# One regrouping transfer per pair instead of per duo, the last pair divided on two engines, half of the last FFN input later, and new orders

## The reference, cut to what matters

```
xn  = layernorm(x)
xa  = layernorm(xn) * ln_w + ln_b
q, k, v = xa @ W_q + b_q, xa @ W_k + b_k, xa @ W_v + b_v      # 16 heads of 64
p   = softmax(causal(q k^T / 8))                               # 256 x 256 per head
att = concat(p v) @ W_o + b_o
ffn = relu(xn @ tern(W1)^T + b1) @ tern(W2)^T + b2             # 512 hidden, weights -1, 0, 1
out = x + att + ffn
```

## Time and profile before

| | us |
|---|---|
| median of 3 runs | 224.38 (223.8 to 224.81) |
| the profiled execution, its own time | 225.33 |
| its span in the trace | 223.5 |
| PE busy | 211.9 (95%) |
| VectorE busy | 201.8 (90%) |
| ScalarE busy | 195.5 (87%) |
| GpSimd busy | 184.8 (83%) |

### The profile page before, as it was taken

The page is one execution under the profiler, slowest core; times in us unless marked ns, Lnnn a source line. Parts: engine busy times, 40 slices in busy tenths (PEclk is TensorE's granted clock), DMA queues, the critical chain, the costliest instruction groups (busy, mean ns, idle before and its releaser), DMA issues.

```text
span 223.5 us, 9672 instructions
## 1 busy us (share of the span) xinstructions
PE 211.9 (95%) x3670; PEld 187.9 (84%) x3670; DVE 201.8 (90%) x776; ACT 195.5 (87%) x733; POOL 184.8 (83%) x363
## 2 busy tenths in 40 slices
PE   7999799999999999999998999989999999999795
PEld 5766498888998899889987999879998998899584
DVE  3499999999999999999999999999999999999931
ACT  0999999997999899997999899997999899996830
POOL 5799989999988989798988899797988985996530
PEclk9999999999999999999999999999999999999999
DMA  5990656606675487636855566636756567677700
GB/s 155 279 273 6 141 116 172 143 3 144 146 158 127 105 196 174 133 78 153 172 134 150 123 147 159 121 84 143 173 119 177 109 152 171 153 165 161 165 5 23
DMA packets 24030, 30.79 MB, mean 138 GB/s; under 512 B 2608, under 2 KB 23088, under 8 KB 23984
## 3 DMA queue, kind: packets, MB, share of 16 engines
q1 hardware_dynamic: 23840, 30.16, 57.5%
q10 hardware_dynamic: 144, 0.02, 0.0%
HBM read 4.73 MB, written 1.05 MB: 26 GB/s over the span
## 4 chain that ended last, share of the span: by engine, by line
PE 46%; ACT 16%; DVE 14%; POOL 11%; DMA 7%; SPq 3%; issue 2%; POOLq 0%; DVEq 0%
PE s_ps L822 8%; DMA pT<-blocks 7%; PE m_ps L862 7%; ACT prob L491 5%; DVE s_ps L603 4%; ACT prob L493 4%; PE m_ps L940 4%; DVE blocks L616 3%; SPq L351 3%; PE m_ps L787 3%; POOL prob L315 3%; ACT qk L480 2%; PE m_ps L789 2%; PE m_ps L788 2%; ACT qk L482 2%; POOL prob L314 2%
## 5 line engine op out<-in xcount | busy, mean ns | idle before, releaser
L491 ACT ACTIVATE prob<-s_ps,neg_max 128x256 f32<-128x256 f32 x128 | 67.6, 528 | 5.6 <-DVE neg_max L603 5.2
L315 POOL TENSOR_SCALAR prob<-prob,inv_sum 128x256 f32<-128x256 f32 x126 | 61.3, 486 | 0.0
L616 DVE STREAM_TRANSPOSE blocks<-prob 128x768 f32<-128x768 f32 x62 | 59.7, 968 | 1.6 <-POOL prob L315 1.6
L314 POOL TENSOR_SCALAR prob<-prob,inv_sum 128x128 f32<-128x128 f32 x126 | 47.5, 377 | 15.4 <-DVE inv_sum L610 15.4
L603 DVE CUSTOM_DVE_ANT_0 s_ps<-s_ps,causal 128x256 f32<-128x256 f32 x128 | 55.1, 430 | 5.0 <-PE s_ps L822 4.5
L493 ACT ACTIVATE prob<-s_ps,neg_max 128x128 f32<-128x128 f32 x128 | 54.0, 422 | 0.0
L862 PE MATMUL m_ps<-pT,v 64*64 64x64 f32 (+2 forms) x1536 | 49.0, 256 | 3.5 <-DMA pT<-blocks 2.1
L822 PE MATMUL s_ps<-qk 64*64 64x128 f32 (+2 forms) x1280 | 49.9, 276 | 0.9 <-ACT prob L493 0.5
L862 PEld LDWEIGHTS m_ps<-pT,v 64*64 64x64 f32 x1536 | 42.5, 133 | 8.8 <-DVE zT_lo L622 3.6
L822 PEld LDWEIGHTS s_ps<-qk 64*64 64x64 f32 x1280 | 42.0, 133 | 7.1 <-issue 3.8
L603 DVE CUSTOM_DVE_ANT_0 s_ps<-s_ps,causal_first 128x128 f32<-128x128 f32 x128 | 42.4, 331 | 0.0
(11 more groups left out here) (120 smaller groups left out, 492.4 us busy)
## 6 DMA issues: line engine op xcount, KB each, us to landing
pT<-blocks SPq DMA_DIRECT2D x124, 192.0 KB, 3.6
xT_cur<-in_xT SPq DMA_DIRECT2D x8, 128.0 KB, 4.2
outT<-out_sb SPq DMA_DIRECT2D x8, 128.0 KB, 4.0
x_all<-in_x SPq DMA_DIRECT2D x1, 768.0 KB, 8.6
wv_raw<-in_w_v SPq DMA_DIRECT2D x2, 256.0 KB, 5.5
wo<-in_w_o SPq DMA_DIRECT2D x1, 512.0 KB, 6.5
x_all<-in_x SPq DMA_DIRECT2D x2, 128.0 KB, 3.9
wq_raw<-in_w_q SPq DMA_DIRECT2D x2, 128.0 KB, 2.5
```

The source lines that it names most:

```text
L314: op(first, first, inv_sum[:, j, 2 + h:3 + h], 0.0, ALU.mult, ALU.add)
L315: last = op(later, later, inv_sum[:, j, h:h + 1], 0.0, ALU.mult, ALU.add)
L491: nc.scalar.activation(later, s_ps[:, pair % 2, h, 0:S].rearrange("p (g j k) -> p g j k", g=TILES, j=QT), ACT.Exp, bias=neg_max[:, j, h:h ...
L616: nc.vector.transpose(blocks[:, duo, :, n, :, :], prob[:, pair % NBUF, :, :, :, :] .rearrange("p h j g k -> p (j g) h k")).then_inc(turned, 1)
```

## The change

Three edits of structure, and new order strings for all five queues.

**A transfer for each pair.** `blocks` and `pT` are laid out by pair instead of by duo, `pT_in` has 8 semaphores, and `regroup(b, pair)` waits for its own pair's turning and issues 4 DMAs of 128 runs of 768 bytes, 96 KB each. A batch then has 32 regrouping DMAs with the same bytes in all. `turn_blocks` waits for its own pair's transfer of the batch before, and `y` waits for both pairs' semaphores. The wait on `z_psd` is the duo's, as before.

**The last pair's division.** `divide_on_vector` (`q7` on VectorE) divides head 0 alone, in 2 instructions, and a new step `q7` on ScalarE, `divide_on_scalar`, divides head 1 in 2 instructions. `tw7` and `tn` wait for both.

**The last FFN input.** In batch 7 `oa` takes hidden chunks 0 and 1 (4 products) and waits for the first half of `h` alone; chunks 2 and 3 enter at the head of `ob`, with the wait for the second half. The number of products is the same.

```diff
-        blocks = sb("blocks", [P, DUOS, QT * 3, 2, 2, QB])
-        pT = sb("pT", [P, DUOS, QT, 3, 2, 2, QB])
+        blocks = sb("blocks", [P, PAIRS, QT * 3, 2, QB])
+        pT = sb("pT", [P, PAIRS, QT, 3, 2, QB])
...
-            def regroup(b, duo):
-                wait(sp, turned, PAIRS * b + 2 * duo + 2)
-                wait(sp, z_psd, 4 * (DUOS * (b - 1) + duo + 1))
+            def regroup(b, pair):
+                wait(sp, turned, PAIRS * b + pair + 1)
+                wait(sp, z_psd, 4 * (DUOS * (b - 1) + pair // 2 + 1))
                 for i in range(QT):
                     rows = slice(i * QB, i * QB + QB)
-                    sp.dma_start(pT[:, duo, i, :, :, :, :].rearrange("p g n h q -> p (g n h q)"),
-                                 blocks[rows, duo, :, :, :, :].rearrange("k c n h q -> k (c n h q)")
-                                 .rearrange("k (j r) -> k j r", j=QT)).then_inc(pT_in[duo], 16)
+                    sp.dma_start(pT[:, pair, i, :, :, :].rearrange("p g h q -> p (g h q)"),
+                                 blocks[rows, pair, :, :, :].rearrange("k c h q -> k (c h q)")
+                                 .rearrange("k (j r) -> k j r", j=QT)).then_inc(pT_in[pair], 16)
...
+            def divide_on_scalar(b, pair):
+                wait(act, inv_ready, PAIRS * b + pair + 1)
+                j = pair % NBUF
+                for cols, col in ((slice(0, P), 3), (slice(P, W), 1)):
+                    part = ordered(pair, 1)[:, cols]
+                    last = nc.scalar.activation(part, part, ACT.Copy, scale=inv_sum[:, j, col:col + 1])
+                last.then_inc(last_prob_by_scalar, 1)
...
-                        pe.wait_ge(pT_in[duo], 16 * QT * (b + 1))
+                        for pair in (2 * duo, 2 * duo + 1):
+                            pe.wait_ge(pT_in[pair], 16 * QT * (b + 1))
...
+            def hidden_into(dst, chunks, clears):
+                for hid in (hT_hi, hT_lo):
+                    for c in chunks:
+                        nc.tensor.matmul(dst, w2T[:, c, :], hid[:, c, :], start=(clears and hid is hT_hi and c == 0), stop=False)
...
-                wait(pe, h_ready, 2 * b + 2)
-                for hid in (hT_hi, hT_lo):
-                    for c in range(FC):
-                        nc.tensor.matmul(dst, w2T[:, c, :], hid[:, c, :], start=(hid is hT_hi and c == 0), stop=False)
+                if b < B - 1:
+                    wait(pe, h_ready, 2 * b + 2)
+                    hidden_into(dst, range(FC), True)
+                else:
+                    wait(pe, h_ready, 2 * b + 1)
+                    hidden_into(dst, range(FC // 2), True)
...
+                if b == B - 1 and duos.start == DUOS // 2:
+                    wait(pe, h_ready, 2 * b + 2)
+                    hidden_into(dst, range(FC // 2, FC), False)
```

**The orders.** The strings of SP and of the repeated and last batch for VectorE, and the tails of ScalarE and TensorE, before and after:

```diff
-DVE_PLAN = ("i7- m0 m1 ln+ m2 z0- t7- m3 i0 m4 m5 z1- i1 t0 v0 m6 i2 m7 z2- m8 m9 v1 t1 i3 m10 m11 z3- v2 t2 m12 "
-            "xh+ t3 i4 m13 i5 v3 m14 m15 t4 i6 t5 xn+ o- t6")
+DVE_PLAN = ("m1 t6- m2 z0- ln+ i0 m3 t7- m4 z1- m5 i1 v0 m6 m7 i2 m8 z2- m9 v1 t0 m10 m11 i3 z3- t1 i4 v2 xh+ m12 "
+            "t2 v3 i5 m13 t3 t4 m14 i6 m15 m0+ t5 xn+ o- i7")
-DVE_TAIL = ("... i5 m13 t4 o- t5 i6 m14 m15 z0 v2 i7 v3 q7 z1 n3 z2 z3 o")
+DVE_TAIL = ("... v1 t4 t5 o- m14 m15 z0 v2 i6 v3 i7 q7 z1 n3 z2 z3 o")
-ACT_TAIL = ("... z0 e14 e15 f0 z1 w6 f1 w7 z2 z3")
+ACT_TAIL = ("... z0 e14 e15 f0 q7 f1 z1 w6 w7 z2 z3")
-PE_TAIL = ("... x1:1 f0:2 y1:0 z1 tw6:3 f1:2 tw7:3 x2:0 tn3:2 y2:1 x3:2 z2 y3:3 z3 oa:1 ob oc")
+PE_TAIL = ("... f0:2 x1:1 y1:0 f1:3 z1 tw6:2 tn3:3 tw7:2 x2:0 y2:1 z2 x3:3 y3:2 z3 oa:0 ob oc")
-SP_HEAD = ("d0 d1 d2 d3 d0+ d1+ d2+ d3+ d0++ st d1++")
-SP_PLAN = ("d2 d3 st- d0+ d1+")
-SP_TAIL = ("d2 st- st")
+SP_HEAD = ("d0 d1 d2 d3 d4 d5 d6 d7 d0+ d1+ d2+ d3+ d4+ d5+ d6+ d7+ st d0++ d1++ d2++ d3++")
+SP_PLAN = ("d4 d5 d6 d7 d0+ st- d1+ d2+ d3+")
+SP_TAIL = ("d4 d5 st- st")
```

More of the change, by code:

```diff
@@ L48 @@
 BUSY = (5, 1)
-PE_HEAD = ("xb:2 pr0:3 pr1:0 xn:2 s0 pr2:1 pr3:0 s1 v0:3 s2 v1:2 ta:3 pr4:0 pr5:1 s3 pr6:3 v2:2 s4 pr7:3 f0:0 s5 "
[3 rows of a table removed]
[L53 to L64, removed]
@@ L74 @@
-POOL_PLAN = ("h0- p7- h1- p0 p1 ln+ p2 p3 xl+ p4 p5 p6")
-POOL_TAIL = ("p7- p0 h0- p1 h1- p2 p3 p4 p5 p6 h0 h1")
-SP_HEAD = ("d0 d1 d2 d3 d0+ d1+ d2+ d3+ d0++ st d1++")
-SP_PLAN = ("d2 d3 st- d0+ d1+")
-SP_TAIL = ("d2 st- st")
+PE_HEAD = ("xb:0 pr0:0 pr1:1 xn:3 s0 pr2:0 s1 v0:2 v1:3 ta:1 pr3:2 s2 v2:0 pr4:3 pr5:2 s3 pr6:0 s4 pr7:2 v3:0 "
[3 rows of a table added]
+PE_PLAN = ("x0-:2 y0-:1 s1 z0- pr4:3 pr5:0 x1-:2 y1-:1 s2 z1- v0:3 pr6:0 x2-:1 y2-:2 s3 z2- s4 pr7:0 v1:3 x3-:1 "
+           "y3-:2 s5 z3- s6 v2:3 v3:0 xh+:2 oa-:1 f0:3 pr0+:2 pr1+:0 f1:3 s7 s0+ xn+:2 ob- pr2+:0 pr3+:3")
@@ new lines @@
+PE_TAIL = ("x0-:1 pr4:2 y0-:0 s1 x1-:3 z0- y1-:2 s2 z1- x2-:1 y2-:0 s3 z2- pr5:3 pr6:2 s4 v0:3 x3-:2 pr7:0 y3-:1 "
+           "s5 z3- s6 oa-:3 v1:0 ob- x0:1 y0:2 s7 z0 v2:0 v3:3 f0:2 x1:1 y1:0 f1:3 z1 tw6:2 tn3:3 tw7:2 x2:0 "
+           "y2:1 z2 x3:3 y3:2 z3 oa:0 ob oc")
+ACT_HEAD = ("wh0 wh1 pr0 wh2 pr1 xn wh3 e0 aa pr2 e1 e2 e3 pr3 e4 wh4 pr4 e5 pr5 pr6 e6 e7 pr7 xh+ e8 e9 xn+ f0 "
+            "e10 f1 e11 pr0+ e12 e13 pr1+ z0 pr2+ e14 e15 e0+ e1+ pr3+ z1 e2+ pr4+ e3+ pr5+ wh5 e4+ z2 e5+ oh "
+            "pr6+ e6+ e7+ pr7+ z3 e8+ xh++ e9+ e10+ e11+ f0+ f1+ e12+ pr0++ e13+ xn++ e14+ pr1++")
@@ new lines @@
+ACT_PLAN = ("e15- pr2 pr3 e0 z0- e1 pr4 e2 pr5 z1- e3 e4 e5 pr6 z2- e6 e7 e8 e9 pr7 z3- e10 xh+ e11 e12 f0 pr0+ "
+            "e13 pr1+ f1 xn+ e14")
+ACT_TAIL = ("e15- e0 pr2 pr3 pr4 e1 z0- e2 e3 z1- e4 e5 z2- pr5 pr6 e6 e7 e8 e9 pr7 e10 z3- e11 e12 e13 z0 e14 "
+            "e15 f0 q7 f1 z1 w6 w7 z2 z3")
+DVE_HEAD = ("lz nh xb m0 m1 xn ln+ wl0 v0 m2 th m3 v1 m4 i0 m5 te0 v2 m6 i1 t0 m7 m8 wl1 i2 m9 i3 v3 t1 m10 xh+ "
[3 rows of a table added]
+DVE_PLAN = ("m1 t6- m2 z0- ln+ i0 m3 t7- m4 z1- m5 i1 v0 m6 m7 i2 m8 z2- m9 v1 t0 m10 m11 i3 z3- t1 i4 v2 xh+ m12 "
+            "t2 v3 i5 m13 t3 t4 m14 i6 m15 m0+ t5 xn+ o- i7")
@@ new lines @@
+DVE_TAIL = ("t6- m1 t7- m2 i0 m3 z0- m4 m5 i1 z1- t0 m6 i2 m7 z2- t1 m8 m9 t2 v0 i3 m10 m11 m12 i4 t3 z3- i5 m13 "
+            "v1 t4 t5 o- m14 m15 z0 v2 i6 v3 i7 q7 z1 n3 z2 z3 o")
+POOL_HEAD = ("hs np wl2 wl3 ln+ p0 wl4 p1 p2 p3 xl+ h0 p4 p5 h1 p6 p7 ln++ wl5 p0+ ol p1+ p2+ p3+ xl++ p4+ p5+ p6+")
+POOL_PLAN = ("h0- p7- p0 ln+ p1 h1- p2 p3 xl+ p4 p5 p6")
+POOL_TAIL = ("p7- h0- p0 h1- p1 p2 p3 p4 p5 p6 h0 h1")
+SP_HEAD = ("d0 d1 d2 d3 d4 d5 d6 d7 d0+ d1+ d2+ d3+ d4+ d5+ d6+ d7+ st d0++ d1++ d2++ d3++")
@@ L203, in attention_ffn_kernel @@
         vec_in = sem("vec_in")
-        pT_in = [sem(f"pT_in{n}") for n in range(DUOS)]
+        pT_in = [sem(f"pT_in{n}") for n in range(PAIRS)]
         out_done = [sem(f"out_done{n}") for n in range(2)]
@@ L226, in attention_ffn_kernel @@
         last_wide = sem("last_wide")
+        last_prob_by_scalar = sem("last_prob_by_scalar")
         out_bias_ready = sem("out_bias_ready")
@@ L546, in _ @@
                     copy_wide(index)
+                elif kind == "q":
+                    divide_on_scalar(b, index)
                 elif kind == "wh":
@@ L613, in turn_blocks @@
                 wait(dve, prob_ready, PAIRS * b + pair + 1)
-                duo, n = divmod(pair, 2)
-                wait(dve, pT_in[duo], 16 * QT * b)
-                nc.vector.transpose(blocks[:, duo, :, n, :, :], prob[:, pair % NBUF, :, :, :, :]
+                wait(dve, pT_in[pair], 16 * QT * b)
+                nc.vector.transpose(blocks[:, pair, :, :, :], prob[:, pair % NBUF, :, :, :, :]
                                     .rearrange("p h j g k -> p (j g) h k")).then_inc(turned, 1)
@@ L631, in divide_on_vector @@
                 j = pair % NBUF
[L632 to L635, removed]
+                for cols, col in ((slice(0, P), 2), (slice(P, W), 0)):
+                    part = ordered(pair, 0)[:, cols]
+                    last = nc.vector.tensor_tensor(part, part, inv_sum[:, j, col:col + 1].broadcast_to(part.shape), ALU.mult)
                 return last
@@ L859, in product @@
                         else:
-                            turned_part = pT[rows, duo, i, tile + queries.start:tile + queries.stop, n, h, :]\
+                            turned_part = pT[rows, 2 * duo + n, i, tile + queries.start:tile + queries.stop, h, :]\
                                 .rearrange("p i g q -> p g i q")
@@ L892, in wait_divided @@
                     pe.wait_ge(last_prob_ready, 1)
+                    pe.wait_ge(last_prob_by_scalar, 1)
                 else:
```

6 lines of the change are left out of this document (1 added, 5 removed), and 12 rows, old and new, of tables (DVE_HEAD, PE_HEAD).

## The result

The changed kernel takes 245.34 us (median of 4 runs, 244.86 to 246.69) against 224.39 for the kernel before on the same chip: ratio 1.094 [1.090, 1.099]. It is 21 us slower. The forecast was 222.2, and the range ended at 228.0. Some executions of a kernel show a lower granted clock and take some per cent longer; ratios compare the others alone.

The account below looks back on a forecast made before the run. It took VectorE and PE as nearly full, VectorE's work of about 24.3 us limiting each batch. Gains 1.3 + 0.7 - 0.3 + 0.5 = 2.2 us off 224.38 gave 222.2 us, range 219.3 to 228.0.

Parts of the forecast that it names:

- Part 1: Regrouping transfers for each pair: pair 7's data land earlier, so `y3` no longer waits; gain 1.3 us.
- I take 2.35: SP's queue: a group of four 96 KB issues takes 2.35 us, with 3.08 kept for the range.
- It just fits: Before `y3`: pair 7's transfer `d7` lands at 34.6 us into the plan, needed at 35.0.
- the rival: SP's queue becomes the bound in every batch: 225.5 to 228 us, full form about 232; chance 0.30.
- The head: Start of the kernel: `wl0` moved behind `ln+`, 0.3 us uncovered; cost +0.3 us, between -1 and +1.5.
- Part 2: New orders in the repeated batches: less VectorE waiting for scores and GpSimd's division; gain 0.7 us, between 0 and 2.1.
- Part 3: The new order at the kernel's start: a loss of 0.3 us, between -1 and +1.5.
- Part 4: The tail: divided pair ready 1.8 us earlier; gain 0.5 us, between 0 and 1.8, a loss if SP is late.
- the sign of its failure: SP's queue: waits for `turned` shrinking from several us to nothing would mean the queue is the bound.

Follow-up runs that it names:

- half the issues: Each pair regrouped in two DMAs of 192 KB (output not the reference's): in the changed kernel 222.56 us, in the kernel before with its own orders 223.76 us.
- Early landings alone: The kernel before with its own orders, each pair regrouped by itself in two DMAs of 192 KB (output not the reference's): 223.76 us, ratio 0.996.
- the tail's experiment: The kernel before with only pair 7's division shared by VectorE and ScalarE and the late FFN half, PE's order as before: 224.14 us, ratio 0.9973.

## Why the prediction was wrong

**Two steps failed. The first is the first term of Part 1, "I take 2.35" us for a group of four issues.** It rested on four issues at the price of the first one, 0.54. But 0.54 is the first issue of a group; one behind another takes 0.60 (median 605 ns of 248). The earlier trace rows had the median, 616 ns, and the prediction quoted only the smallest. A group is 2.51 without any hold, 2.81 on the average of the run, and 2.76 to 3.06, gaps included, on the average of the seven in a row. The half that was right: the growth of the issues to 1.1 us within a group was a backlog, and with 96 KB it is gone.

**"It just fits"** was then a sum without room: `d7` landing at 34.6 where 35.0 was the need. It named its own limit, 2.5 us a group, and the median measured is 2.51 (the shortest 2.48, the mean 2.81).

**The second step is the overlap: the rival was the case, but its price was too small.** It decided from 2.94 us a group, eight groups and SP's other work in 25.2 us. The groups measured, 2.90 on the average of the four rows of the loop, stay below that, and by the prediction's own rule they give 225.5 to 228, not 245. The old orders with the same transfers come near that (229.5), though by the first two batches and the end and not by waits in each. The rule treats SP as an engine with a share of work, and has nothing for a new order in which SP's work waits for `y3` and `y3` for SP's work. The loop decides earlier: from `y3` to pair 1's issue 4.3 us at best, seven groups, 1.9 to the next `y3`. It fits 25.2 us up to (25.2 - 4.3 - 1.9) / 7 = 2.71 us a group. At 3.0 it gives 27.2, and with 5.8 instead of 4.3 it gives 28.7: 2 to 3.5 us a batch, not the 1.2 of the prediction (the rows of the loop have 0.3 to 3.0). The difference is the part that waits for SP and then makes SP wait: PE takes its steps in order, and the scores behind `y3` and VectorE's `z3-` ahead of `t1` stand behind the landing.

**The head** was costed at +0.3, between -1 and +1.5; it lost 8.3. SP issues from 25.14 to 46.1 without a pause in batch 0 and from 57.55 to 78.25 in batch 1: the prediction counted SP's work in the repeated batches only. With half the issues the head has nothing of it: `y3` of batches 0 and 1 comes at 44.9 and 70.8, 0.7 and 1.0 us sooner than before.

**The sum of the gains was right for a kernel whose queue is free, in part by luck.** Early landings alone bring 0.9 us (224.68 x (1 - 0.9958)), forecast 1.3. The tail's edits bring 0.6, forecast 0.5. All together bring 224.68 x (1 - 0.9919) = 1.8, forecast 2.2; if the gains add, which no run shows, 0.3 is left for the orders and the head, forecast 0.4. But it doesn't lie where it was forecast. By the table above the new orders bring nothing in the repeated batches (99.9 us against 99.3), where Part 2 had 0.7, and 1.2 us up to `y3` of batch 1 (70.8 against 72.0), where Part 3 had a loss of 0.3.

**The tail** went as told up to the divided pair. VectorE and ScalarE in the changed kernel, then PE:

```profile
230.61 0.84 ACT L503 ACTIVATE prob<-prob,inv_sum 128x128 f32<-128x128 f32 x2
```

```profile
230.11 0.18 DVE L621 RECIPROCAL inv_sum<-row_sum 128x4 f32<-128x4 f32 x1
230.32 0.67 DVE L645 TENSOR_TENSOR prob<-prob,inv_sum 128x128 f32<-128x128 f32 x2
```

```profile
232.23 0.65 PE L920 MATMUL m_ps<-ident,prob 128*128 128x128 f32 x4
233.20 0.33 PE L912 MATMUL m_ps<-ident,prob 128*128 128x128 f32 x1 [0.32 <-ACT pT L508]
...
234.73 0.79 PE L872 MATMUL m_ps<-pT,v 64*64 64x256 f32 x20 [0.88 <-DMA pT<-blocks]
```

`tn` runs ahead, `tw7` waits 0.32 us for ScalarE's `w6`. From the reciprocals to `y2` it is 4.62 us, before 208.87 to 213.44, 4.57. What takes the early division back is the last row: `y2` waits another 0.88 us for pair 5's transfer, late by SP's queue, the wait that Part 4 named as a loss if SP is late. With the same tail and half the issues the transfer is there, and `y2` follows `tw7` at once, 3.68 us behind the reciprocals (207.36 to 211.04):

```profile
211.04 0.78 PE L872 MATMUL m_ps<-pT,v 64*64 64x256 f32 x20
```

In the tail's experiment, with the old bank order and `w6` ahead of `f1`, it is 4.24 (208.25 to 212.49), the last 0.26 of it again a wait for the transfer.

**What would have shown it beforehand** is how long SP waits for turned blocks in the whole run (us, times, longest), before and after:

```profile
SPq L351 <- DVE blocks L616: 89.2, 31, 11.5
```

```profile
SPq L352 <- DVE blocks L626: 35.9, 20, 9.8
```

62 groups of 2.51 us instead of 31 of 3.08 are 60 us more of queue. With the holds it is 77: the groups sum to 174.1 us, before to 97.3. SP had 89.2 us to spare, and 11.5 of them lay ahead of the first group. The prediction named this row as the sign of its failure, and made no use of what the trace before had for it.

## What to carry to other kernels

Count a queue's issues, not its bytes: price an issue behind another one at the median of the trace and not at the smallest, and compare the added queue time with the time that the queue now waits. Then look for the loop that closes through the queue (landing, the product, the copy, the turning, the next issue) and add up its latency; here it decided at 2.71 us a group, where the queue's own share reached 100% at 2.94. Whether such a loop is there is a matter of the orders: with the old ones the same full queue cost the repeated batches nothing. An order written for early data costs more than it brings when the data come at the old time, so the two are to be tried apart and together.

## What the runs showed that was not expected

**An issue on SP costs about 0.6 us whether it carries 4 KB, 96 KB or 192 KB** (medians 0.56, 0.60 and 0.62; each makes 144 packets, and a number of packets other than that was not tried). With 192 KB four in a row reach 3.0 to 3.1 us, with 96 KB 2.51. The median time from an issue to its landing fell from 3.6 us to 2.4 with half the bytes. The Trainium skill ("DMA: Bandwidth & Descriptors", Anatomy of one DMA) fits, for DMAs from GpSimd's queue, about 2 us and bytes over 436 GB/s. By that an estimate for the 96 KB less is 0.2 us; the trace shows 1.2, for SP's queue and with several of them side by side. The Trainium skill's advice to coalesce many small transfers ("DMA: Bandwidth & Descriptors", Rules for kernel authors), which it gives above all for those under 64 KB, held here at 96 KB for another reason than the landing: the issuing queue.

**Holds of 1 to 2 us** in an issue are there in every kernel of this case (1.68 in the earlier trace rows, 2.06 after). Regrouping issues of over 1.2 us, more than the 1.0 to 1.1 of a fourth issue of 192 KB, are 16 of 248 after, 8 of 124 before, and 5 and 1 of 124 in the two kernels with half the issues a pair. After the change each of the 16 begins within 0.3 us of a packet of the instruction queue q8, of which the profile's page counts few:

```profile
q8 instruction: 29, 0.48, 0.8%
```

If they belong together, the number of holds goes by how much of the time SP is issuing. No experiment here tried whether the one causes the other.

**VectorE and GpSimd met once.** In the head of the changed kernel a ternary product with two inputs in SBUF ran beside GpSimd's low part of W_o:

```profile
46.02 2.35 POOL L466 TENSOR_TENSOR wo_lo<-wo,wo_hi 128x1024 fp32r<-128x1024 f32 x1 [0.55 <-ACT wo_hi L564]
46.20 2.72 DVE L589 SCALAR_TENSOR_TENSOR w2T<-w2T_raw,thr,out_sb 128x512 fp32r<-128x512 f32 x1
```

Alone, the same instruction took 0.75 us before. It ends at 48.92, 0.55 behind GpSimd's end at 48.37. The Trainium skill ("SBUF — State Buffer", SBUF: two separate sides) states that such a pair takes a shared port as an exclusive lock, the one that starts first keeping it for the whole instruction; this row agrees. It cost nothing visible here, since VectorE's next step then waited 1.15 us for scores, but it is 2 us that an order alone can bring about. In the kernel with the new orders and half the issues the same step ended before GpSimd's began, and took 0.75.
